# Moving two kinds of copies from VectorE to ScalarE in a post-norm attention and FFN layer

## The reference, cut to what matters

```python
qkv = x @ W_qkv.T + b_qkv                      # q is then scaled by 64 ** -0.5
attn = softmax(einsum('bhnld,bhnmd->bhnlm', qb, kb))      # blocks of L = 64 tokens
out = einsum('bhnlm,bhnmd->bhnld', attn, vb)
x = layernorm(x + (out @ W_out.T + b_out))
h = silu(x @ wg.T) * (x @ wu.T)                # wg, wu, wd: int * (1 / 127)
x = layernorm(x + h @ wd.T)
```

## Time and profile before

| | us |
|---|---|
| time before, median of 2 runs | 2707.83 |
| the two runs | 2686.14 and 2729.51 |
| the profiled execution, its own time | 2686.38 |
| its span on the slowest core | 2684.8 |
| spans of the eight cores | 2658.8 to 2684.8 |

### The profile page before, as it was taken

The page is one execution under the profiler, slowest core; times in us unless marked ns, Lnnn a source line. Parts: engine busy times, 40 slices in busy tenths (PEclk is TensorE's granted clock), DMA queues, the critical chain, the costliest instruction groups (busy, mean ns, idle before and its releaser), DMA issues.

```text
span 2684.8 us, 27480 instructions; the slowest of 8 cores (2658.8 to 2684.8 us)
## 1 busy us (share of the span) xinstructions
PE 1999.2 (74%) x10560; PEld 1000.3 (37%) x10560; DVE 816.7 (30%) x1314; ACT 434.2 (16%) x835; POOL 67.1 (3%) x111
## 2 busy tenths in 40 slices
PE   1567209866798678976798678977698678977796
PEld 1333204323443344433443244434443244434342
DVE  2444001043312432143412532133411542133421
ACT  0111101012211122112211122112211122112110
POOL 2000000100000000000000000000000000000000
PEclk9967659978799679978799679978799678977798
DMA  9999995640054102510044102520044102520033
GB/s 183 163 110 120 192 244 167 132 118 32 16 150 127 37 17 87 165 63 32 16 141 126 47 16 86 158 71 32 16 141 125 48 16 69 167 79 16 23 119 110
DMA packets 260174, 253.55 MB, mean 94 GB/s; under 512 B 89952, under 2 KB 223088, under 8 KB 259472
## 3 DMA queue, kind: packets, MB, share of 16 engines
q1 hardware_dynamic: 216576, 121.65, 17.7%
q0 software_dynamic: 19280, 86.11, 14.7%
q10 hardware_dynamic: 24192, 44.05, 5.3%
HBM read 216.13 MB, written 56.62 MB: 102 GB/s over the span
## 4 chain that ended last, share of the span: by engine, by line
PE 60%; DVE 15%; SPq 9%; DMA 5%; issue 4%; another core or an unknown queue 3%; ACT 3%; DVEq 0%; POOL 0%; ACTq 0%; POOLq 0%
PE ps L787 25%; PE ps L842 10%; SPq L289 8%; PE ps L392 7%; PE ps L582 6%; PE ps L426 3%; DMA wdb<-wd_nat 2%; PE ps L475 2%; PE ps L469 2%; DVE diag L511 2%; DVE stats L494 2%; DVE attnT L542 2%; SPq L263 2%; DVE x L863 1%
## 5 line engine op out<-in xcount | busy, mean ns | idle before, releaser
L787 PE MATMUL ps<-x1T,wgu 128*128 128x512 bf16 x3072 | 670.9, 381 | 108.8 <-DMA wgu<-wuT_s 107.3
L787 PEld LDWEIGHTS ps<-x1T,wgu 128*128 128x128 bf16 x3072 | 301.8, 98 | 475.2 <-issue 118.4
L805 DVE TENSOR_TENSOR hT<-silu,ps 128x512 bf16<-128x512 bf16 x192 | 132.1, 688 | 749.6 <-PE ps L787 642.1
L842 PE MATMUL ps<-wdb,hT 128*128 128x512 bf16 x1536 | 340.4, 383 | 25.7 <-DMA wdb<-wd_nat 17.3
L392 PE MATMUL ps<-xT,RWqkv 128*128 128x256 bf16 x2048 | 250.1, 287 | 1.6 <-DVE xT L373 1.5
L842 PEld LDWEIGHTS ps<-wdb,hT 128*128 128x128 bf16 x1536 | 149.5, 98 | 216.5 <-issue 44.2
L392 PEld LDWEIGHTS ps<-xT,RWqkv 128*128 128x128 bf16 x2048 | 196.9, 103 | 52.1 <-issue 2.1
L426 PE MATMUL ps<-RWqkv,xT 128*128 128x512 bf16 x512 | 154.0, 455 | 79.6 <-ACT ps L878 42.1
L582 PE MATMUL ps<-RWout,aoT 128*128 128x512 bf16 x512 | 180.2, 515 | 35.1 <-DVE aoT L570 35.1
L799 ACT ACTIVATE silu<-ps 128x512 bf16<-128x512 f32 x192 | 114.6, 597 | 521.2 <-PE ps L787 521.1
L400 ACT ACTIVATE qkT<-ps,bqkvT_s 128x256 bf16<-128x256 f32 x256 | 121.5, 474 | 325.9 <-PE ps L392 325.8
(11 more groups left out here) (71 smaller groups left out, 1069.4 us busy)
## 6 DMA issues: line engine op xcount, KB each, us to landing
wgu<-wgT_s SPq DMA_DIRECT2D x64, 768.0 KB, 4.8
wgu<-wuT_s SPq DMA_DIRECT2D x64, 768.0 KB, 6.8
wdb<-wdT_s ACTq DMA_DIRECT2D x168, 256.0 KB, 2.6
xf<-x POOLq DMA_DIRECT2D x16, 1024.0 KB, 5.2
y<-x POOLq DMA_DIRECT2D x16, 1024.0 KB, 5.5
x<-wqkv POOLq DMA_DIRECT2D x24, 512.0 KB, 8.3
wg_nat<-wg POOLq DMA_DIRECT2D x1, 6144.0 KB, 64.2
wu_nat<-wu POOLq DMA_DIRECT2D x1, 6144.0 KB, 122.3
```

Source lines behind the costliest of these rows:

```text
L787: P.do("tensor", lambda tn, wi=wi, k=k, mi_=mi_, boff=boff, pair=pair: tn.matmul(pair[:, wi * 512:(wi + 1) * 512], wgu[:, boff + wi * (KCH ...
L805: P.do("vector", lambda v, m=m, pair=pair: v.tensor_tensor(hT[:, m * 512:(m + 1) * 512], silu2[:, (m % 2) * 512:(m % 2 + 1) * 512], pair[: ...
L842: P.do("tensor", lambda tn, m=m, l=l, half=half, wslot=wslot, coff=coff: tn.matmul(psl[l][:, half * 512:(half + 1) * 512], hT[:, m * 512 + ...
```

## The change

Two kinds of copies go from VectorE (`tensor_copy`) to ScalarE (`activation` with `Copy`): the copy of the attention output from PSUM to `aoT` (line 570, four in a tile) and the copy of the normalised half to bf16 (line 704, two in a tile). The waits of those who read them, and the hand-over of the PSUM banks, follow from `ve` to `sc`. The wait of the second kind on `norm1` was one of VectorE on itself and becomes one of ScalarE on VectorE.

```diff
-                        P.do("vector", lambda v, st=st, hh=hh, bank=bank: v.tensor_copy(
+                        P.do("scalar", lambda sC, st=st, hh=hh, bank=bank: sC.activation(
                             out=aoT[:, hh * 4 * 256:(hh + 1) * 4 * 256].rearrange(
                                 "p (c j) -> p c j", j=256)[:, :, st * 128:st * 128 + 128],
-                            in_=ps01[:, bank * 512:(bank + 1) * 512].rearrange("p (c j) -> p c j", j=128)),
-                            inc="ve", waits=[("pe", mil["out", t, st, hh])])
-                        mil["aoT", t, st, hh] = P.c["ve"]
-                        P.rel("ps01_" + str(bank), "ve")
+                            in_=ps01[:, bank * 512:(bank + 1) * 512].rearrange("p (c j) -> p c j", j=128),
+                            func=AF.Copy),
+                            inc="sc", waits=[("pe", mil["out", t, st, hh])])
+                        mil["aoT", t, st, hh] = P.c["sc"]
+                        P.rel("ps01_" + str(bank), "sc")
...
-                    w = P.acq("ps23") + [("ve", mil["aoT", t, st, 1]), ("sc", mil["bcast"]), ("sp3", mil["rwout"])]
+                    w = P.acq("ps23") + [("sc", mil["aoT", t, st, 1]), ("sc", mil["bcast"]), ("sp3", mil["rwout"])]
...
-                    P.do("vector", lambda v, xsl=xsl, st=st: v.tensor_copy(
-                        out=aoT[:, st * 1024:(st + 1) * 1024], in_=xsl),
-                        inc="ve",
-                        waits=[("ve!", mil["norm1", t, st]), ("pe", mil["wout", t, 1]),
+                    P.do("scalar", lambda sC, xsl=xsl, st=st: sC.activation(
+                        out=aoT[:, st * 1024:(st + 1) * 1024], in_=xsl, func=AF.Copy),
+                        inc="sc",
+                        waits=[("ve", mil["norm1", t, st]), ("pe", mil["wout", t, 1]),
                                ("sb5", mil.get("dump_aoT", 0))])
-                    mil["x1b", t, st] = P.c["ve"]
+                    mil["x1b", t, st] = P.c["sc"]
...
-                            waits=(w + [("ve", mil["x1b", t, st])]) if c == 0 else ())
+                            waits=(w + [("sc", mil["x1b", t, st])]) if c == 0 else ())
```

More of the change, by code:

```diff
@@ L636, in tile_front @@
                     P.do("gpsimd", lambda q: q.dma_start(out=dbg_t["d_aoT"], in_=aoT[:]),
-                         inc="sb5", amt=16, waits=[("ve", mil["aoT", DBG_T, 1, 1])])
+                         inc="sb5", amt=16, waits=[("sc", mil["aoT", DBG_T, 1, 1])])
                     mil["dump_aoT"] = 16
@@ L838, in ffn @@
                         w += P.acq("ps01_0") + P.acq("ps01_1") + P.acq("ps23") + P.acq("ps45") + P.acq("ps67")
-                        w += [("ve", mil["aoT", 2 * s + 1, 1, 1]), ("ve", mil["x1t_evac", 2 * s + 1, 1])]
+                        w += [("sc", mil["aoT", 2 * s + 1, 1, 1]), ("ve", mil["x1t_evac", 2 * s + 1, 1])]
                     for l in range(4):
```

## The result

The changed kernel takes 0.9935 of the time of the kernel before (95% interval 0.9918 to 0.9953). That is 0.65% less, some 17 us: within 2%. Its median is 2666.6 us, against 2685.45 for the kernel before in the same comparison, and lies inside the range. Some runs of each kernel are slow by some per cent; these two medians include them, while the ratios and all other times and profiles here are of fast runs. The forecast was 2656.9 us, 29.5 us less. About six tenths of the forecast gain arrived.

What follows compares the result with a forecast made beforehand. No engine was short of time; TensorE's waits for other engines bound 14 of 16 tiles. Saved waits of 1.24 + 0.09 + 0.78 = 2.11 us a tile, times 14, take 29.5 us from 2686.4: 2656.9 us, range 2632 to 2690.

Steps and rivals of the forecast that it cites:

- The first projection: TensorE's wait before it, set by line 570's copy, goes entirely once ScalarE copies: 1.24 us a tile.
- the second: Second projection's wait for line 570's copy shrinks only by the shorter copy: 0.09 us a tile.
- The transposes: Waits before both transposes of the normalised halves shrink with line 704's copies on ScalarE: 0.78 us a tile.
- The second transposes' part: They wait only for VectorE to empty `ps23`, no longer a copy: 1.48 us instead of 2.08, 0.60 gained.
- The first transposes: ScalarE's slower copy starts 0.11 us after the first normalisation, without waiting for the second: 0.18 us gained.
- What the copies cost: On ScalarE, line 570's copy was taken at 0.60 us and line 704's at 1.05 us.
- I take the middle, in which the rise moves with the work: TensorE's clock rises shift with the earlier starts, so the summed 29.5 us holds; forecast chance 0.48.
- Rival 1: TensorE's clock rises stay put in time: only 8.8 us gained, 2677.6 us; chance 0.22.
- Rival 2: Clock rises come sooner, the first projection's 3.4 us after its start: 41 us gained, 2645.1 us; chance 0.23.
- Rival 3: Copies cost what they cost and nothing overlaps: 0.56 us a tile slower, 7.8 in all, 2694.2 us; chance 0.04.
- Rival 4: ScalarE loads tables for copies and exponents, about four a tile on the path: 72 us, 2728.9 us; chance 0.03.

Runs made afterwards that it cites:

- e3: Kernel before, with two small VectorE steps repeated in each tile's first layer norm, on the chain the transposes wait for; 2688.27 us.
- e11: Kernel of e5 plus 32 unread matmuls a tile in TensorE's wait between second projection and first transposes; 2611.29 us.
- e1: Kernel before with only the copies of line 570 moved to ScalarE; ratio 0.9958 to the kernel before.
- e2: Kernel before with only the copies of line 704 moved to ScalarE; ratio 1.000 to the kernel before.
- e12: Kernel of e9 with 32 unread matmuls a tile instead of 20; ratio 0.9549 to the kernel before.
- e7: Changed kernel with nine small VectorE steps added in each tile's layer norm, with the lines of e4; 2699.73 us.
- e4: Kernel before, with nine small VectorE steps repeated in each tile's first layer norm, on the chain the transposes wait for; 2726.38 us.
- e10: Changed kernel with two PSUM banks each for line 713's and the input's transposes, and every second attnT copy on ScalarE; ratio 0.9611 to the kernel before.
- e5: Changed kernel with the second half's transposes of line 713 in another PSUM bank, so they need not wait for the first evacuation; 2641.28 us.
- e9: Kernel of e10 plus 20 unread matmuls a tile in the wait ahead of line 713's transposes; ratio 0.9602 to the kernel before.

## Why the prediction was right, and where it was not

- The first projection, 1.24 us, and the second, 0.09: right. 1.33 us a tile was forecast, 1.36 measured; the second was to wait 0.83 us (0.94 - 0.09 is 0.85) and waits 0.84.
- The transposes, 0.78 us: mis-sized, 0.54 measured, 0.21 us a tile too much in all, or 2.9 us over 14 tiles. The second transposes' part holds (1.58 us left, 1.48 forecast). The first transposes, which should have gained 0.18, stand at 121.8 / 16 = 7.61 us in the mean, the value of the earlier trace rows. They gain 0.13 us in the odd tiles (7.48) and lose up to 0.41 in the even ones from the third group on; in the one shown, ScalarE's copy starts later than the 0.11 us that the step allowed.
- What the copies cost: right, 593 and 1048 ns.
- The step that failed is the clock's, "I take the middle, in which the rise moves with the work". 1.90 us a tile over 14 tiles are 26.6 us; some 17 arrived, so about 9 us were given back. The ratio's interval stands for 12.6 to 22.0 us of gain, so these 9 are good to some 5; the two profiles put it at 10.2. That the loss is with the clock is shown by the queries, the same matmuls, which are busy 12.5 us longer, by the rises, by e3, where half a us a tile more costs nothing, and by e11, where the clock alone moved the time.
- Rival 1, in which the rises stay put, had the mechanism of the even tile shown. Its end was wrong. It let what is left over vanish in each tile (8.8 us in all). In truth a group gives up 3.4 us at once when enough has come together: 34 groups of 40 did so here, 12 in e1, 1 in e2. In the odd tiles the rise of the first projection did not stay put either, but moved by 3.4 us. That is why two parts worth 0.42% and nothing make 0.65%, and why the result lies between rival 1 and the forecast.
- Rival 2, rises sooner: seen, but it did not pay. In the even tile the first projection comes up 5.7 us after its start, in place of 5.2, though the pause before it is gone. In the odd tile it comes up after 3.0 us, about the 3.4 that the rival had, and is 0.81 us shorter, about its 0.85. The rival left out what follows: the second projection then comes up later and is 1.08 us longer, and the queries 0.94. The Trainium skill (TensorE: Matmul & The Clock Gate, "Loop structure matters more than you think") has it that matmuls without pauses between them stay warm. The change took away one short pause and left that of 8.02 us; only e11 and e12, which filled that one too, show the rule at work, with queries of 14.16 us.
- Rival 3, op for op: fell. ScalarE's two copies stand back to back, and no wait became longer by their 1048 ns. The Trainium skill's rule (Perfetto Trace Analysis, "Optimizing Scalar/DVE Operations"), to hand a copy over where VectorE is saturated, agrees in the durations of the copies of line 704 (685 and 1048 ns); those of line 570 are shorter on ScalarE (593 against 684 ns). It would have kept the former on VectorE, at 30%; the measurement decides against that here, since together with the other kind they bring more groups to the shorter time than that kind alone (34 of 40 against 12).
- Rival 4, table loads: fell, 17 as before.
- That the time lies inside the range says little for the middle reading of the clock: the range held rivals 1 and 2 as well. It came out between them because a rise that came sooner in the odd tiles and the losses behind it stood against each other, which no step had foreseen. That part is luck.

Open are the later copies of the even tiles, why the groups of e7, e11 and e12 spread where those of e4 do not, and what e10 gains beyond its waits.

## What to carry to other kernels

Ask first behind what a copy stands, then what it costs: two copies of 1048 ns on an engine that had nothing to do served their reader better than two of 685 ns in a queue. Where TensorE falls to 1.2 GHz and comes up again several times in a loop, don't multiply saved wait by the number of tiles: look whether the rises move with the work, measure the loop's own time from one round to the next, and try small savings together, since each alone may be worth nothing. If a wait can't be removed, compare the time with the wait filled up to the next dense stretch: a filling that stopped short of it brought little or nothing here.

## What had not been expected of the hardware

The clock's rises in the even tile kept their distances to 0.01 us (34.13, 10.25, 17.06) while the matmuls between them moved by half a us; in the odd tile one of them moved by 3.4 us at once. With that, 0.6 us a tile less waiting (e2) and 0.48 us more (e3) both left a group's time as it was, and 2.4 us more (e4) cost either 3.4 or 6.8 us a group, but not 4.85. And TensorE gained by work that nobody reads: 32 unread matmuls a tile took 4.3 us off a group in one kernel (e11 against e5) and 1.6 in another (e12 against e10), where 20 took nothing (e9 against e10).
